# Adapter matmul and quantised FFN: weight units cut by outputs, loop turned by half a period, first two and last sequences re-ordered

## The chip, the cores and the metric

One core of a Trainium2 chip runs the whole kernel. The metric is device time in microseconds (us), from one launch to its end. The core has five engines that run their own instruction streams and meet at semaphores: PE (matmuls; PEld is its weight load), DVE, ACT and POOL (element work), and SP, which here only issues DMAs. SP's queue is in order: an issue that waits holds up all issues behind it.

## What is computed

Eight sequences of 256 tokens, width 1024. Each has its own adapter matrix (1024 x 1024, float32, picked by `itok_B_1_14`), and all share one FFN:

```python
y = einsum('bij,bkj->bik', x, weight[ids])          # adapter: 4 MB of weights per sequence
h = layernorm(y, gamma, beta)
h = fake_quant_int8(h) @ fake_quant_int8(w1).T + b1 # scale per row, round, clip
h = gelu(h)
h = fake_quant_int8(h) @ fake_quant_int8(w3).T + b3
return x + h
```

`fake_quant_int8` divides a row by max|row|/127, rounds, and multiplies back.

## The kernel before

**Adapter matmul.** A float32 product is made of three fp32r matmuls (hi\*hi, lo\*hi, hi\*lo), after both operands are split: `hi` is the value rounded by an ACT copy, `lo` = value - `hi` by DVE (weights) or POOL (tokens). The weights of a sequence come in four units `u` = 0 to 3. `divmod(u, 2)` is `(kh, ch)`: which 512 outputs, which 512 inputs. A unit is 512 outputs x 512 inputs, loaded by four DMAs (`load_unit`, one for 32 partitions each, rows of 128 floats = 512 bytes) into one of two slots of `w_nat`. DVE transposes it in 32 x 32 blocks into PSUM (`transpose_w`, L801) in two pieces `k`, ACT writes `w_hi` (`split_w`, L537), DVE writes `w_lo` (`low_w`, L807), and PE runs piece (u, k): 12 matmuls of 128x512 (`piece`, `products`, L1080 to L1082). The first piece of unit 2 can run when the first piece of that unit is split. Tokens go the same way: `load_x`, `transpose_x` (L816), `split_x`, `low_x` (POOL, L438).

**FFN.** It runs on 128-token tiles t = 0, 1: `copy_y`, `statistics`, `normalisers` (POOL), `normalise` (ACT), `scale_and_shift` (POOL, L413 and L415), `scales_h` (DVE), `round_h` (ACT), `transpose_h` (PE), `take_h`, `ffn1` (16 bf16 matmuls), `rescale1` (DVE, L874), `add_b1` (POOL), `gelu`, `scales_g`, `round_g`, `transpose_g`, `take_g`, `ffn2`, `scale_ffn2` (ACT, L585), `finish` (POOL, L421 and L424), `store`. The products of h and g, and the transposes, share the two banks `f_ps`.

**Preparation.** w1 and w3 are 16 tiles of 128 rows ("prep tiles"), each loaded (`load_prep`), reduced to a row maximum (`max_prep`), rounded (`round_prep`: POOL for tiles 0 to 5, ACT for 6 to 15), transposed by PE (`prepare`) and copied (`take_prep`). The tiles lie in buffers that are borrowed, so some loads wait: tile 13 until 8 tiles are transposed, tiles 14 and 15 until h of sequence 0 is rounded.

**Order.** Everything is written out by hand for each engine. Sequence 0 is transposed by PE (`transpose_first`), not by DVE. Sequences 1 and 2 are written out with the preparation between their pieces. Then a loop over p = 3 to 6 (period p): PE runs units 0 and 1 of sequence p with `ffn2` of p-2 (first half), then units 2 and 3 with `ffn1` of p-1 (second half). DVE and ACT prepare weights half a period ahead: units 2 and 3 of p in the first half, units 0 and 1 of p+1 in the second. Sequence 7 is `last_period`, token tile 0 through all units and then tile 1, before the FFNs of 6 and 7.

In the period SP issues: units 0 and 1 of p+1, store of tile 0, unit 2, store of tile 1, the residual tokens (`load_residual`), tokens of p+2, unit 3. A unit's slot is free when the unit two before it is transposed. A store waits for POOL's `finish`.

## Time and profile before

| | |
|---|---|
| median of 3 runs | 408.69 us (406.43 to 411.79) |
| the profiled execution, device time | 405.16 us |
| its span, first to last instruction | 403.3 us |
| mean granted PE clock | 0.954 of full speed |
| bytes moved | 67.35 MB, mean 167 GB/s |

The profile is of one execution. "Busy" of PE is modelled at its end: matmuls overlap, so the distance between two starts is what one costs, not its printed duration. A row of a timeline is: start, duration, engine, line, operation, tiles, and in brackets how long the engine stood idle before it and on whom it waited.

### The profile page before, as it was taken

The page shows a single profiled execution, that of the slowest core. Times are in us where ns is not written, and L with a number is a line of the kernel's source. Part 1 is how long each engine was busy: PE and PEld are TensorE (multiplying, and loading weights), DVE is VectorE, ACT ScalarE, POOL GpSimd, SP SyncE. Part 2 cuts the span into 40 slices and gives each one's busy share as a digit, 9 for nine tenths or more (in the row PEclk, how much of TensorE's full clock was granted, in tenths as well). Part 3 has the DMA queues.
Part 4 walks back from the last instruction along what each step waited for, and adds up shares of the span by engine and source line. Part 5 has one row for each costly group of instructions (what it writes and reads, how often), then busy time and mean ns, then how long its engine had stood idle before and what let it go on. Part 6 is the DMA issues. An engine that isn't in the chain of part 4 may idle for free. (4 is left out here: it accounts for less than half of the span.)

```text
span 403.3 us, 5528 instructions
## 1 busy us (share of the span) xinstructions
PE 340.1 (84%) x1760; PEld 229.2 (57%) x1760; DVE 292.8 (73%) x348; ACT 237.7 (59%) x248; POOL 266.8 (66%) x160
## 2 busy tenths in 40 slices
PE   3999883988558847899999999999999899992973
PEld 3788663656445533566666666566556566741331
DVE  1489693998776354699768986997689886457457
ACT  2345593858866343786687667756775865214360
POOL 1406334657900647996999699968996899585454
PEclk9999999799888969999999999999999999996898
DMA  7999999964840519999985896689569801300004
GB/s 258 364 265 298 222 283 235 212 160 142 171 105 0 138 20 244 215 191 233 269 154 104 248 250 126 156 257 204 110 156 271 197 0 54 119 37 2 0 27 181
DMA packets 78619, 67.35 MB, mean 167 GB/s; under 512 B 3078, under 2 KB 71686, under 8 KB 78602
## 3 DMA queue, kind: packets, MB, share of 16 engines
q1 hardware_dynamic: 78602, 67.14, 68.9%
q8 instruction: 9, 0.15, 0.2%
q14 instruction: 8, 0.07, 0.1%
HBM read 58.74 MB, written 8.39 MB: 166 GB/s over the span
## 5 line engine op out<-in xcount | busy, mean ns | idle before, releaser
L1080 PE MATMUL a_ps<-w_hi,x_hi 128*128 128x512 f32 x240 | 104.3, 435 | 10.8 <-DVE w_lo L807 8.1
L1129 PE MATMUL f_ps<-w_q,q_t 128*128 128x512 bf16 x416 | 94.3, 380 | 4.9 <-ACT q_t L580 2.7
L1081 PE MATMUL a_ps<-w_lo,x_hi 128*128 128x512 f32 x240 | 96.6, 402 | 0.0
L1082 PE MATMUL a_ps<-w_hi,x_lo 128*128 128x512 f32 x240 | 96.5, 402 | 0.0
L801 DVE STREAM_TRANSPOSE t_ps<-w_nat 128x1024 f32<-128x1024 f32 x56 | 67.3, 1236 | 19.4 <-DMA w_nat<-in_L_cond_weight 19.0
L807 DVE TENSOR_TENSOR w_lo<-t_ps,w_hi 128x1024 fp32r<-128x1024 f32 x56 | 66.9, 1216 | 12.9 <-ACT w_hi L537 12.6
L537 ACT ACTIVATE w_hi<-t_ps 128x1024 fp32r<-128x1024 f32 x56 | 57.1, 1024 | 23.5 <-DVE t_ps L801 22.5
L1129 PEld LDWEIGHTS f_ps<-w_q,q_t 128*128 128x128 bf16 x416 | 38.7, 98 | 55.1 <-issue 4.7
L1080 PEld LDWEIGHTS a_ps<-w_hi,x_hi 128*128 128x128 f32 x240 | 47.1, 196 | 23.9 <-DVE w_lo L807 9.0
L1082 PEld LDWEIGHTS a_ps<-w_hi,x_lo 128*128 128x128 f32 x240 | 46.8, 195 | 10.7
L1081 PEld LDWEIGHTS a_ps<-w_lo,x_hi 128*128 128x128 f32 x240 | 47.2, 197 | 8.7
L438 POOL TENSOR_TENSOR x_lo<-x_t,x_hi 128x1024 fp32r<-128x1024 f32 x14 | 33.5, 2390 | 26.0 <-ACT x_hi L543 26.0
L421 POOL TENSOR_TENSOR o<-o,w_scale_row 128x1024 f32<-128x1024 f32 x12 | 29.6, 2468 | 31.3 <-ACT o L585 31.3
L429 POOL TENSOR_TENSOR x_res<-x_res,rows 128x1024 f32<-128x1024 f32 x14 | 33.9, 2446 | 10.1 <-DMA x_res<-in_x 10.0
L433 POOL TENSOR_TENSOR a<-a,rows 128x1024 f32<-128x1024 f32 x14 | 34.4, 2459 | 8.2 <-DVE a L874 8.2
L850 DVE TENSOR_REDUCE g_max<-a 128x1 f32<-128x1024 f32 x14 | 17.1, 1218 | 18.1 <-ACT a L571 18.1
L424 POOL TENSOR_TENSOR o<-o,x_res 128x1024 f32<-128x1024 f32 x12 | 28.6, 2388 | 0.9
L415 POOL TENSOR_TENSOR y<-y,rows 128x1024 f32<-128x1024 f32 x12 | 28.6, 2386 | 0.9
L413 POOL TENSOR_TENSOR y<-y,rows 128x1024 f32<-128x1024 f32 x12 | 28.6, 2384 | 0.8 <-ACT y L556 0.8
L543 ACT ACTIVATE x_hi<-x_t 128x1024 fp32r<-128x1024 f32 x14 | 14.7, 1052 | 16.0 <-DVE x_t L816 10.6
L842 DVE TENSOR_REDUCE h_max<-y 128x1 f32<-128x1024 f32 x14 | 17.0, 1213 | 9.6 <-POOL y L415 9.6
L575 ACT ACTIVATE a<-a,magic,g_inv 128x1024 f32<-128x1024 f32 x14 | 17.4, 1245 | 10.7 <-DVE g_inv L838 10.7
(143 smaller groups left out, 488.8 us busy)
## 6 DMA issues: line engine op xcount, KB each, us to landing
w_nat<-in_L_cond_weight SPq DMA_DIRECT2D x112, 256.0 KB, 5.5
x_nat<-in_x SPq DMA_DIRECT2D x28, 256.0 KB, 8.1
x_res<-in_x SPq DMA_DIRECT2D x7, 1024.0 KB, 6.9
out<-o SPq DMA_DIRECT2D x14, 512.0 KB, 2.9
w_nat<-in_L_cond_weight SPq DMA_DIRECT2D x4, 512.0 KB, 6.5
w_q<-in_L_ffn_w SPq DMA_DIRECT2D x4, 512.0 KB, 8.7
w_scale_row<-in_L_ffn_w SPq DMA_DIRECT2D x3, 512.0 KB, 9.8
o<-in_x SPq DMA_DIRECT2D x2, 512.0 KB, 4.4
```

Source lines behind the costliest of these rows:

```text
L413: pool.tensor_tensor(row, row, gamma_row, ALU.mult).then_inc(gamma_done, 1)
L421: pool.tensor_tensor(o[:, t, :], o[:, t, :], w_scale_row[:, 1, :], ALU.mult).then_inc(out_scaled, 1)
L429: pool.tensor_tensor(x_res[:, t, :], x_res[:, t, :], b3_row, ALU.add).then_inc(x_b3_ready, 1)
L433: pool.tensor_tensor(a[:, t, :], a[:, t, :], b1_row, ALU.add).then_inc(ffn1_biased, 1)
L438: pool.tensor_tensor(x_lo[:, half], x_t[:, half], x_hi[:, half].bitcast(F32), ALU.subtract).then_inc(x_lo_ready, 1)
L537: act.activation(w_hi[:, u, blocks_of(k)], t_ps[:, k], ACT.Copy).then_inc(w_hi_ready, 1)
L801: dve.transpose(t_ps[:, k].rearrange("p c (kb s) -> p kb c s", s=BLK), w_nat[:, u % 2].rearrange("p kb (c r) -> p kb c r", r=BLK)[:, :, bl ...
L807: dve.tensor_tensor(w_lo[:, u, blocks_of(k)], t_ps[:, k], w_hi[:, u, blocks_of(k)].bitcast(F32), ALU.subtract).then_inc(w_lo_ready, 1)
L1080: pe.matmul(ps, hi, w_hi[:, u, c], start=begin, stop=False)
L1081: pe.matmul(ps, hi, w_lo[:, u, c], start=False, stop=False)
L1082: last = pe.matmul(ps, lo, w_hi[:, u, c], start=False, stop=end)
L1129: last = pe.matmul(ps[:, half, :], q[:, c, :], w[:, c, half_of(half)], start=c == 0, stop=c == CB - 1)
```

## The change

1. **Units cut by outputs.** A unit is now 256 outputs x all 1024 inputs (`LOADED = 256`), still 1 MB in four DMAs, with rows of 256 floats = 1 KB. A piece `k` of it is one half of the inputs. So what PE calls unit (kh, ch) is filled by two loaded units, 2\*kh and 2\*kh+1, and PE waits before it for piece `ch` of the second of them.
2. **Loop turned.** The body begins with the second half: p = 2 to 6, PE runs units 2 and 3 of p with `ffn1` of p-1, then units 0 and 1 of p+1 with `ffn2` of p-1. All engines follow. In SP's cycle the load of unit 1 now stands behind the store of tile 0, and the load of unit 2 behind the residual.
3. **First sequences.** `ffn1` of sequence 0 runs in the first half of sequence 1 (before: in its second half and after), `ffn2` of 0 in the first half of sequence 2 (before: its second). Prep tiles 3 to 8 are transposed between sequences 0 and 1. All rounding is POOL's. The loads are in another order (diff).
4. **Last sequence.** Units 0 and 1 of sequence 7 run in the loop. What is left runs tile 0, tile 1, and the products of 6 and 7 are cut in halves that alternate with transposes. POOL adds b3 to the residual of 6 after `add_b1`, no longer before it. The rounding of h and g of sequence 7 is ACT's, before DVE's.

```diff
-    NK = 2
-    CP = CU // NK
-    PIECES = UNITS * NK
+    CP = CU // 2
+    LOADS = 4
+    PIECES = LOADS * CH
+    LOADED = D // LOADS
+    KB = LOADED // BLK
...
+        def part_of_unit(w, u, k):
+            kh, quarter = divmod(u, LOADS // KH)
+            return w[:, CH * kh + k, :, quarter * LOADED:(quarter + 1) * LOADED]
...
                 for q in range(NQ):
-                    j0 = q * JX + ch * JQ
-                    src = weight[bass.ds(adapter, 1), kh * BANK:(kh + 1) * BANK, j0:j0 + JQ]
+                    src = weight[bass.ds(adapter, 1), u * LOADED:(u + 1) * LOADED, q * JX:(q + 1) * JX]
...
             def period(p):
-                load_unit(p + 1, 0)
-                load_unit(p + 1, 1)
-                store(p - 2, 0)
+                load_residual(p - 1)
                 load_unit(p + 1, 2)
-                store(p - 2, 1)
-                load_residual(p - 1)
                 if not (isinstance(p, int) and p + 2 > LAST):
                     load_x(p + 2)
                 load_unit(p + 1, 3)
+                if not (isinstance(p, int) and p + 2 > LAST):
+                    load_unit(p + 2, 0)
+                store(p - 1, 0)
+                if not (isinstance(p, int) and p + 2 > LAST):
+                    load_unit(p + 2, 1)
+                store(p - 1, 1)
...
             load_first_unit(2)
-            load_first_unit(3)
-            load_prep(range(0, 4))
+            load_prep((0,))
+            load_first_unit(3, (0,))
+            load_prep((1, 2, 5, 3))
             load_x(1)
+            load_first_unit(3, (1,))
+            load_prep((7, 4, 12, 8, 6))
+            load_unit(1, 1)
+            load_prep((9,))
             load_unit(1, 0)
...
+            load_prep((10,))
+            load_x(2)
+            load_prep((11, 13))
             load_unit(1, 2)
...
+            load_prep((14,))
             load_unit(1, 3)
-            load_prep(range(13, 14))
+            load_prep((15,))
+            load_unit(2, 1)
             load_unit(2, 0)
...
             def piece(b, u, k):
+                kh, ch = divmod(u, CH)
...
-                    pe.wait_ge(w_lo_ready, piece_no(b, u, k) + 1)
-                    if u < CH and k == 0:
-                        pe.wait_ge(x_lo_ready, CH * (b - 1) + u + 1)
...
+                elif k == 0:
+                    pe.wait_ge(w_lo_ready, piece_no(b, 2 * kh + 1, ch) + 1)
+                    if kh == 0:
+                        pe.wait_ge(x_lo_ready, CH * (b - 1) + ch + 1)
```

Three places of the order. **SP in the loop, before**: the store of tile 0 (`out<-o`), behind which stands unit 2 of the next sequence.

```order
L321 ISA [waits out_ready]
L321 DMA out<-o 128x1024
L256 TENSOR_LOAD ids_sb
L256 ISA x2
L261 REGISTER_ALU
L266 ISA [waits w_transposed]
L266 DMA w_nat<-in_L_cond_weight 32x16x128
```

**SP in the loop, after**: the same store; what stands behind it is unit 1.

```order
L330 REGISTER_ALU
L332 DMA out<-o 128x1024 [waits out_ready]
L265 TENSOR_LOAD ids_sb
L265 ISA x2
L273 ISA [waits w_transposed]
L273 DMA w_nat<-in_L_cond_weight 32x8x256
```

The load of unit 1 has moved behind a wait for POOL (`out_ready`); the shape of a DMA went from 16 blocks x 128 floats to 8 x 256.

**SP before the loop, after the change**: prep tile 13 with its wait for 8 transposed tiles, and unit 2 of sequence 1 behind it.

```order
L327 DMA o<-in_L_ffn_w 128x1024 [waits first_transposed]
L327 DMA w_scale_row<-in_L_ffn_w 128x1024 [waits wq_transposed]
L265 TENSOR_LOAD ids_sb
L265 ISA x2
L273 ISA [waits w_transposed]
L273 DMA w_nat<-in_L_cond_weight 32x8x256
```

In the kernel before, unit 2 of sequence 1 stood ahead of that tile.

**DVE before the first half of sequence 2, before** (`w_loaded0` and `w_loaded1` are the two slots): unit 0's second piece, then unit 1.

```order
L801 STREAM_TRANSPOSE t_ps<-w_nat 128x16x2x32 [waits w_lo_ready,w_loaded0]
L824 BN_STATS stats<-y 128x6 [waits y_copied] x2
L874 SCALAR_TENSOR_TENSOR a<-f_ps,h_scale,w_scale_row 128x512 [waits ffn1_done,scale_row_ready]
L874 SCALAR_TENSOR_TENSOR a<-f_ps,h_scale,w_scale_row 128x512 [waits ffn1_done]
L831 BN_AGGR mean_var<-stats 128x2 [waits shift_ready,y_stats,consts_ready]
L831 BN_AGGR mean_var<-stats 128x2
L807 TENSOR_TENSOR w_lo<-t_ps,w_hi 128x1024 [waits w_hi_ready]
L801 STREAM_TRANSPOSE t_ps<-w_nat 128x16x2x32 [waits w_lo_ready,w_loaded1]
```

**DVE at the same place, after**: from the first transpose of unit 0 of sequence 2 to the third `w_lo` (the one PE waits for).

```order
L763 STREAM_TRANSPOSE t_ps<-w_nat 128x8x4x32 [waits w_lo_ready,w_loaded0]
L778 STREAM_TRANSPOSE x_t<-x_nat 128x8x8x32 [waits x_lo_ready,x_loaded]
L763 STREAM_TRANSPOSE t_ps<-w_nat 128x8x4x32 [waits w_lo_ready,w_loaded0]
L769 TENSOR_TENSOR w_lo<-t_ps,w_hi 128x4x256 [waits w_hi_ready]
L763 STREAM_TRANSPOSE t_ps<-w_nat 128x8x4x32 [waits w_lo_ready,w_loaded1]
L769 TENSOR_TENSOR w_lo<-t_ps,w_hi 128x4x256 [waits w_hi_ready]
L812 TENSOR_REDUCE g_max<-a 128x1 [waits g_ready]
L798 TENSOR_SCALAR g_scale<-g_max 128x1 [waits g_max_ready]
L800 RECIPROCAL g_inv<-g_scale 128x1 [waits g_scale_ready]
L786 BN_STATS stats<-y 128x6 [waits mean_var_ready,y_copied] x2
L769 TENSOR_TENSOR w_lo<-t_ps,w_hi 128x4x256 [waits w_hi_ready]
```

The token transpose of sequence 2 now stands inside the weight chain, and three `w_lo` instead of one stand before the first piece of the half.

## Rows read from the trace of the kernel before

**Rows 1.** The page: span, busy time of each engine.
```profile
span 403.3 us, 5528 instructions
PE 340.1 (84%) x1760; PEld 229.2 (57%) x1760; DVE 292.8 (73%) x348; ACT 237.7 (59%) x248; POOL 266.8 (66%) x160
```
**Rows 2.** Windows: start:end, length, busy per engine, PE clock, DMA share, GB/s.
```profile
0.00:43.92 43.92, 35.60 (x208) 30.15 (x209) 27.98 (x25) 20.38 (x24) 13.22 (x22) 1.00 1.04 289
43.92:161.73 117.81, 86.71 (x449) 59.92 (x449) 80.69 (x98) 72.72 (x76) 59.55 (x34) 0.90 0.70 160
161.73:317.78 156.05, 152.96 (x770) 101.01 (x769) 129.33 (x158) 109.84 (x113) 136.06 (x72) 1.00 0.88 197
317.78:403.30 85.52, 64.83 (x338) 38.16 (x336) 54.81 (x70) 34.79 (x37) 57.99 (x34) 0.92 0.16 59
182.05:201.01 18.96, 18.96 (x99) 12.66 (x97) 16.21 (x20) 12.43 (x13) 14.76 (x9) 1.00 1.00 254
277.90:298.90 21.00, 19.49 (x98) 12.51 (x96) 15.02 (x20) 14.85 (x17) 20.62 (x13) 1.00 0.71 133
```
**Rows 3.** PE's timeline at two waits and after them (matmul starts).
```profile
71.15 0.79 PE L1080 MATMUL a_ps<-w_hi,x_hi 128*128 128x512 f32 x1 [5.23 <-DVE w_lo L807]
72.17 0.63 PE L1082 MATMUL a_ps<-w_hi,x_lo 128*128 128x512 f32 x1
72.60 0.63 PE L1080 MATMUL a_ps<-w_hi,x_hi 128*128 128x512 f32 x1
121.05 0.77 PE L1080 MATMUL a_ps<-w_hi,x_hi 128*128 128x512 f32 x1 [0.44 <-ACT y L552]
146.83 1.01 PE L1105 MATMUL f_ps<-ident,h_r 128*128 128x128 bf16 x8 [7.02 <-ACT o L585]
230.21 0.39 PE L1082 MATMUL a_ps<-w_hi,x_lo 128*128 128x512 f32 x1
230.44 0.40 PE L1080 MATMUL a_ps<-w_hi,x_hi 128*128 128x512 f32 x1
232.50 0.62 PE L1105 MATMUL f_ps<-ident,h_r 128*128 128x128 bf16 x8
```
**Rows 4.** SP's and DVE's timelines: a store, unit 1 behind it, its transpose.
```profile
135.01 0.37 SPq L321 DMA_DIRECT2D out<-o  x1
136.14 2.00 SPq L266 DMA_DIRECT2D w_nat<-in_L_cond_weight  x4
143.37 1.26 DVE L801 STREAM_TRANSPOSE t_ps<-w_nat 128x1024 f32<-128x1024 f32 x1 [8.68 <-DMA w_nat<-in_L_cond_weight]
```
**Rows 5.** DMA packets in the stretches 0:20, 10:15, 20:22, 23.5:28.5, 29:33 us.
```profile
DMA packets 5024, 6.19 MB, mean 310 GB/s; under 512 B 184, under 2 KB 4280, under 8 KB 5024
DMA packets 1751, 1.74 MB, mean 349 GB/s; under 512 B 61, under 2 KB 1747, under 8 KB 1751
DMA packets 228, 0.82 MB, mean 410 GB/s; under 512 B 28, under 2 KB 28, under 8 KB 228
DMA packets 1253, 1.08 MB, mean 216 GB/s; under 512 B 66, under 2 KB 1250, under 8 KB 1252
DMA packets 1548, 0.85 MB, mean 213 GB/s; under 512 B 50, under 2 KB 1525, under 8 KB 1548
```
**Rows 6.** DVE's timeline in the loop: `w_lo` of units 3, transposes of unit 1, rescale.
```profile
217.81 2.35 DVE L807 TENSOR_TENSOR w_lo<-t_ps,w_hi 128x1024 fp32r<-128x1024 f32 x2
228.19 2.34 DVE L801 STREAM_TRANSPOSE t_ps<-w_nat 128x1024 f32<-128x1024 f32 x2
230.44 1.37 DVE L874 SCALAR_TENSOR_TENSOR a<-f_ps,h_scale,w_scale_row 128x512 f32<-128x512 f32 x2
```
**Rows 7.** POOL's timeline in the same period: the end of `finish` of tile 0.
```profile
218.64 2.37 POOL L424 TENSOR_TENSOR o<-o,x_res 128x1024 f32<-128x1024 f32 x1
```
**Rows 8.** POOL's timeline at the end: the residual of 6, then `add_b1`.
```profile
354.56 5.64 POOL L429 TENSOR_TENSOR x_res<-x_res,rows 128x1024 f32<-128x1024 f32 x2 [6.37 <-DMA x_res<-in_x]
361.27 3.33 POOL L433 TENSOR_TENSOR a<-a,rows 128x1024 f32<-128x1024 f32 x1
```

709 lines of the change are left out of this document (305 added, 404 removed).

## The prediction, made before the changed kernel ran

> **What bounds the kernel now.** I first read the page and then windows cut where PE starts a sequence. PE is busy 84% of the span and no other engine more than 73% [rows 1], but that is a mean over four stages [rows 2]. 0 to 43.9: sequence 0, filled by DMA. 43.9 to 161.7: sequences 1 and 2 among the preparation, 117.8 us with PE busy 86.7 and a granted clock of 0.90. 161.7 to 317.8: the loop, four periods in 156.1 us, PE busy 153.0. 317.8 to 403.3: the last sequence and the last FFNs, 85.5 us with PE busy 64.8.
>
> The loop has little to give. An undisturbed half period is 18.96 us [rows 2], four products and four transposes of FFN and 48 matmuls at the distance of two starts, 0.23 us [rows 3]. Four periods at 2 x 18.96 are 151.7; 156.1 were measured, so all waits of the loop are 4.4 us. The gain or loss of this change has to come from the second and fourth stage. There PE waits for DVE's `w_lo`, and DVE for loads: 5.23 us at 71.15, and 7.02 at 146.83 [rows 3]. The second is a chain through SP's queue: the store of sequence 0 goes out at 135.01, unit 1 of sequence 3 behind it at 136.14, and its transpose starts at 143.37 after 8.68 us of idle DVE [rows 4]. After such waits PE's clock is at its lower level (1.2 GHz): two matmuls start 0.43 us apart (72.17 and 72.60) where 0.23 is usual (230.21 and 230.44) [rows 3]. Over the 12 matmuls of a piece that is 2.4 us, so a wait of 5 us costs 7.4.
>
> **The 1 KB runs.** Here the title's first item is weighed. In 23.5 to 28.5 us the queue moved tokens, whose form is exactly that of the new weight loads (32 partitions, 8 blocks of 256 floats): 216 GB/s. In 29 to 33 us it moved weight units in 512-byte runs: 213 GB/s. Runs of 1 KB to 128 partitions (10 to 15 us) went at 349, and prep tiles in 4 KB rows at 410 (20 to 22) [rows 5]. The new loads stay with 32 partitions per DMA, so I take the row of the same form: 1.05 MB at 216 GB/s is 4.9 us a unit, as before (4.9). The bound on the other side is 349 GB/s, 3.0 us. From issue to transpose an isolated unit takes 7.2 us (136.14 to 143.37) [rows 4], 2.0 of it issuing.
>
> The Trainium skill, page "DMA: Bandwidth & Descriptors", section Specifications, gives 512 B as the smallest transfer for line rate, so by it too going from 512 B to 1 KB buys nothing. By the page the sum below stands as it is; by the 349 row it would be some 6 us lower, which is a rival below. The trace agrees with the page for loads of this form (216 against 213), not for what is line rate: 4 KB rows went at twice that.
>
> **The first sequences, step by step.** Before 20 us about the same bytes go out (6.19 MB) [rows 5]. Then the new queue holds, ahead of and including unit 0 of sequence 1: prep 5 and 3 (0.52 MB each, 1.28 us at 410), tokens (4.9), half a first unit (1.5 at 349), five prep tiles (6.4), unit 1 (4.9), prep 9 (1.3), unit 0 (4.9). That is 26.5 us, so unit 0 has landed at about 47.5 with 1 us of latency. Unit 0 used to come before four of those tiles, so sequence 1 starts later than at 43.9. PE needs three `w_lo`: DVE does three transposes and three `w_lo` at 1.17 each (two in 2.34 or 2.35) [rows 6] and 1.5 of statistics: 47.5 + 8.5 = 56.0. Between, PE transposes prep tiles 3 to 8. The clock is then low: +2.4.
>
> The first half of sequence 1 now carries `ffn1` of 0: 18.96 + 0.9 for the scale row + 2.4 = 22.3, to 78.3. The second half is four pieces of 2.75 (12 x 0.23) = 11.0, with seven prep transposes of 0.45 and a scale row: 15.1, to 93.4. But DVE is late for sequence 2. From 56.0 it has five transposes and three `w_lo` (9.4), three prep maxima (3.5), two `scales_h` (3.0), a rescale and a scale (1.8), and about 0.8 of waiting for units, until unit 3 of sequence 1 is transposed at 74.5. Only then is SP let on to unit 1 of sequence 2, and unit 0 stands behind it although its slot has been free: 74.5 + 1.3 + 2 x 4.9 = 85.6, about 86. From there to the third `w_lo` the order shows three weight transposes and three `w_lo` (7.0), the token transpose (2.3), `scales_g` (1.5) and statistics (1.3): 12.1. PE starts sequence 2 at 98.2, after 5 us of idling, again at the low clock. With `ffn2` of 0 inside, the half takes 18.96 + 2.4, and I add 0.9 for hand-overs: the second half of sequence 2 starts at **120.5**. POOL, which now rounds all tiles, is not the limit in this sum: beside the rounding it has 20 instructions of some 2.4 us [rows 7] between 45 and 120, and its tightest point, `low_x` of sequence 2, comes out at 95.6 against 98.2.
>
> Before, PE reached that place at 121.05 [rows 3]. The same time, but in another state: `ffn2` of 0 is done, and the loop is entered. From 121.05 the old kernel needs 40.7 us to the start of sequence 3 at 161.73. The new one needs a half period, 18.96 + 0.4: sequence 3 starts at 139.9. **First part: -21.8 us.**
>
> **The loop.** All engines keep their cyclic order, with two exceptions. PE's first piece of unit 2 waits for a third `w_lo` instead of a first. Before, that `w_lo` (the first of the pair that starts at 217.81 [rows 6]) was done at 219.0, and PE came to the place at 219.97, the end of a half of 18.96 from 201.01 [rows 2]: 1.0 us to spare, so it costs nothing, but nothing is left as cover. Second, unit 1 stands behind the store of tile 0. POOL's `finish` ends at 221.01 [rows 7]; with 0.4 for the store and 7.2 to the transpose, unit 1 is there at 228.6, and DVE wants it at 228.19 [rows 6]. The transposes, then the rescale, slip 0.4 to 0.7; the rescale ended at 231.8 and PE wants the bank at 232.50 [rows 3, 6], so most of it is swallowed. In front of the residual unit 1 takes the place of unit 2, so the residual lands no later. I take 39.4 for a period, 0.4 over the 39.0 measured: four periods 157.6 against 156.1, sequence 7 starts at 297.5. **+1.5 us.** Bounds: 37.9 a period (-4.5) and 42.0, twice the worst half [rows 2] (+12).
>
> **The last stage.** It was 85.5 us. POOL's queue stood 6.37 us for the residual of 6 and spent 5.64 on it [rows 8], ahead of the normalisers of the last tile and of `add_b1` (361.27), on which both FFNs hung: 12.0, now moved behind. The halved products that alternate with transposes I count at 1.0. 85.5 - 13.0 = 72.5. **-13.0 us.** Bounds: 0, if something else arrives as late as POOL did, and -20.7, all of the stage's time with PE idle.
>
> **Sum.** 403.3 - 21.8 + 1.5 - 13.0 = 370.0 us of span. Around the span lie 1.9 us (405.16 device time), so 371.9, a ratio of 0.918 to that execution. The median of the runs is 408.69, so I expect **375 us**.
>
> **Rivals.**
> *Unit 1 behind the store paces the loop* (0.18). Then POOL's `finish`, the landing, the rescale and PE's transpose form a ring, and the 0.4 to 0.7 of each period adds up with the missing cover before unit 2: a half of 21.0 occurred [rows 2]. At 2 us per period over mine, five periods in all: +10, **385 us**. For it: the ring made the 7.02 us wait. Against it: in the loop only 0.4 us are missing.
> *The new runs go at 349 GB/s* (0.12). A unit takes 1.9 us less. Two units lie in a row before sequence 2 (-3.8, to which the low clock adds), and unit 1 is in time in the loop (-1.6): **369 us**. Against it: the token row.
> *The gain in front is lost again* (0.06). The new order is right only if each engine finds its operands; the old one lost 31 us of PE in its second stage. If the ordered queues lose 20 us of the 21.8, it ends near **396**, and a little more gives no change.
> *Slower* (0.03). A unit takes long from issue to transpose because of its 32-partition form. The price is paid at each load behind a released slot: four in front and one in each of five periods. It decides from 4.6 us each: 9 x 4.6 = 41 over 375 is 2% above 408.69. Against it: 7.2 us were measured where the queue was free, and the queue is 12% idle in the loop [rows 2]. **420 us**.
>
> **How the numbers follow.** The forecast has 0.61 and by itself 367 to 383: the loop's lower bound, and 8 us for steps left out of the hand-made chain. To hold 8 in 10 the range takes in both nearer rivals: 364 to 392. About 2% is what a measurement can tell from no change. Faster by over 2% means below 400.5: forecast, the first two rivals, and two thirds of the third, 0.93, less a little for a mechanism I don't see: 0.91. Same 0.05, slower 0.04.
>
> **What would show it.** Right: unit loads still near 215 GB/s; sequence 1 starts near 56 and sequence 2 near 98, each after a wait for `w_lo` and with matmuls 0.43 apart; sequence 3 near 140; periods of 39 to 40; a last stage of 72 without POOL waiting for a residual. Wrong: a `w_nat` load that DVE waits for in every period, PE waiting for `w_lo` ahead of unit 2 each time, or POOL busy without a gap from 45 to 120 with PE waiting for `x_lo`.

## The result, and the profile after

The changed kernel takes 390.5 us (median of 4 runs, 390.23 to 393.73), the kernel before 409.07 in the same comparison: a ratio of 0.956, 95% interval 0.948 to 0.964. Its profiled execution took 390.59 with a span of 388.7. The direction held, and so did the range (364 to 392), by 1.5 us; 375 was expected. The forecast of the span was 370.0, so 18.7 us of the gain of 33.3 did not come. For the runs below: on the chip of t1, d1 and d2 the kernel before took 403.3 to 415.3 us, and seven of its eleven executions there were in a slower state at a lower granted clock, so the record calls the ratios of these three unclear. The page of after, against [rows 1]:

```profile
span 388.7 us, 5553 instructions
PE 336.1 (86%) x1732; PEld 227.5 (59%) x1760; DVE 287.2 (74%) x345; ACT 230.0 (59%) x241; POOL 278.2 (72%) x170
```

The busy times moved little: PE 4.0 us less, DVE 5.6 less, ACT 7.7 less and POOL 11.4 more, since all the rounding of the preparation is now POOL's. Nearly the same work stands closer together. The windows are cut at the same places as [rows 2] (start of sequence 1, 3 and 7); columns: start:end, length, busy per engine with counts, PE clock, DMA share, GB/s.

```profile
0.00:64.91 64.91, 42.23 (x249) 35.01 (x249) 36.51 (x38) 26.48 (x29) 22.94 (x33) 0.90 1.01 259
64.91:150.62 85.71, 76.99 (x406) 53.96 (x409) 69.84 (x84) 56.99 (x62) 60.78 (x33) 0.96 0.76 179
150.62:309.90 159.28, 153.22 (x755) 100.95 (x769) 128.77 (x157) 107.93 (x113) 137.23 (x73) 1.00 0.80 185
309.90:388.70 78.80, 63.62 (x332) 37.55 (x336) 52.05 (x69) 38.60 (x40) 57.25 (x34) 0.94 0.21 72
```

| | before | forecast | measured | off by |
|---|---|---|---|---|
| sequence 3 starts | 161.73 | 139.9 | 150.62 | +10.7 |
| four periods | 156.05 | 157.6 | 159.28 | +1.7 |
| last stage | 85.5 | 72.5 | 78.8 | +6.3 |

So the first part gave 11.1 where 21.8 was forecast, the loop lost 3.2 where 1.5 was, and the last stage gave 6.7 where 13.0 was. I read each of the three.

**The front.** PE's and DVE's timelines around the start of sequence 1 (forecast: unit 0 landed at 47.5, start 56.0):

```profile
58.99 1.01 PE L1044 MATMUL f_ps<-ident,w_scale_row 128*128 128x128 bf16 x8 [8.39 <-ACT w_q L598]
64.14 1.01 PE L1044 MATMUL f_ps<-ident,a 128*128 128x128 bf16 x8 [1.99 <-ACT w_q L598]
64.91 0.77 PE L1018 MATMUL a_ps<-w_hi,x_hi 128*128 128x512 f32 x1
66.33 0.63 PE L1018 MATMUL a_ps<-w_hi,x_hi 128*128 128x512 f32 x1
66.76 0.63 PE L1019 MATMUL a_ps<-w_lo,x_hi 128*128 128x512 f32 x1
55.61 1.26 DVE L763 STREAM_TRANSPOSE t_ps<-w_nat 128x1024 f32<-128x1024 f32 x1 [3.94 <-DMA w_nat<-in_L_cond_weight]
61.93 2.41 DVE L769 TENSOR_TENSOR w_lo<-t_ps,w_hi 128x1024 fp32r<-128x1024 f32 x2
```

Unit 0 of sequence 1 comes at 55.61, 8.1 us late, and the start is 8.9 late. PE's printed wait is not for `w_lo` but for a prep tile that ACT should copy (8.39). The third `w_lo` is done at 64.34 (61.93 + 2.41), 0.6 before the start, so the rows alone don't say which of the two chains holds. The matmuls behind it are 0.43 apart (66.33, 66.76), PE's lower level of 1.2 GHz, as before [rows 3].

The next sequence, in SP's and DVE's timelines:

```profile
86.99 4.39 SPq L273 DMA_DIRECT2D w_nat<-in_L_cond_weight  x8
99.07 1.26 DVE L763 STREAM_TRANSPOSE t_ps<-w_nat 128x1024 f32<-128x1024 f32 x1 [4.92 <-DMA w_nat<-in_L_cond_weight]
```

Units 1 and 0 of sequence 2 go out together at 86.99, in the sum at 74.5, and the transpose of unit 0 comes 12.1 us behind; 11.5 was the sum. Sequence 2 starts at 111.11, forecast 98.2. These 12.9 us are 8.9 at the start of sequence 1, 3.6 from there to the transpose of its unit 3 (22.1 us in place of 18.5) and 0.4 behind it. The 3.6 are waits of DVE for units 2 and 3 (1.81 at 71.04, 2.89 at 82.99; 0.8 in the sum). SP and DVE, for unit 3:

```profile
72.86 0.36 SPq L327 DMA_DIRECT2D y_first<-in_L_ffn_w  x1
73.97 1.81 SPq L273 DMA_DIRECT2D w_nat<-in_L_cond_weight  x4
82.99 1.26 DVE L763 STREAM_TRANSPOSE t_ps<-w_nat 128x1024 f32<-128x1024 f32 x1 [2.89 <-DMA w_nat<-in_L_cond_weight]
```

The slot of unit 3 is free at 65.5, when unit 1 is transposed. Its load goes out only at 73.97, because prep tile 14 (72.86) stands ahead of it in SP's queue and waits until the first tile of h of sequence 0 is rounded (done at 72.83).

**The loop.** One period, SP, DVE and PE (compare [rows 4] and [rows 6]):

```profile
252.08 1.84 SPq L273 DMA_DIRECT2D w_nat<-in_L_cond_weight  x4
259.94 2.39 DVE L763 STREAM_TRANSPOSE t_ps<-w_nat 128x1024 f32<-128x1024 f32 x2 [1.77 <-DMA w_nat<-in_L_cond_weight]
262.24 1.37 DVE L836 SCALAR_TENSOR_TENSOR a<-f_ps,h_scale,w_scale_row 128x512 f32<-128x512 f32 x2
263.66 0.62 PE L1044 MATMUL f_ps<-ident,h_r 128*128 128x128 bf16 x8 [1.10 <-DVE a L836]
```

Unit 1 goes out behind the store, is there 7.9 us later (7.2 in the sum), DVE has waited 1.77, the rescale slips and PE waits 1.10. The store itself left 1.14 us ahead of the unit (250.94; the sum had 0.4 between them). This is the worst of the four periods: in the other three the unit is there after 7.3 us, DVE waits 1.2 and PE 0.5. The 1.1 behind the store is the same in all.

**The last stage.** DVE, POOL, PE and ACT:

```profile
339.44 1.30 DVE L881 SCALAR_TENSOR_TENSOR y<-y,rstd,rows 128x1024 f32<-128x1024 f32 x1 [0.66 <-POOL rstd L407]
346.15 3.32 POOL L441 TENSOR_TENSOR a<-a,rows 128x1024 f32<-128x1024 f32 x1
347.30 3.25 DVE L881 SCALAR_TENSOR_TENSOR y<-y,rstd,rows 128x1024 f32<-128x1024 f32 x1
353.52 0.62 PE L1044 MATMUL a_ps<-ident,h_r 128*128 128x128 bf16 x8 [2.62 <-ACT h_r L568]
356.23 1.04 ACT L577 ACTIVATE a<-a 128x1024 f32<-128x1024 f32 x1
362.32 1.21 DVE L812 TENSOR_REDUCE g_max<-a 128x1 f32<-128x1024 f32 x1
365.25 0.62 PE L1044 MATMUL t_ps<-ident,a 128*128 128x128 bf16 x8 [3.75 <-ACT a L581]
```

POOL waits for no residual of 6 any more, and the bias that stood behind it comes 36.3 us into the stage (346.15 from 309.90), before 43.5 (361.27 [rows 8] from 317.78). That is 7.2 us and not 12.0. From that bias to the end it is 42.6 us, before 42.0, so the halved products gave nothing. PE waits twice behind the bias: 2.62 for `h_r`, where DVE's step on y took 3.25 in place of 1.30 beside POOL, and 3.75 for g, where the GELU was done at 357.3 and DVE took its maximum at 362.32, behind four operations of its queue.

### The profile page after: what moved, and what is told of

Its sections match the earlier page's. It is cut to its first block, busy times and chain, and to the rows that moved or that the text cites. A ratio compares the mean times of both kernels' runs of the same rounds, so it can differ in the third digit from the quotient of the medians.

```text
span 388.7 us, 5553 instructions
## 1 busy us (share of the span) xinstructions
PE 336.1 (86%) x1732; PEld 227.5 (59%) x1760; DVE 287.2 (74%) x345; ACT 230.0 (59%) x241; POOL 278.2 (72%) x170
## 3 DMA queue, kind: packets, MB, share of 16 engines
HBM read 58.74 MB, written 8.39 MB: 173 GB/s over the span
## 4 chain that ended last, share of the span: by engine, by line
POOL 38%; issue 16%; PE 8%; DVE 6%; ACT 2%; POOLq 0%; ACTq 0%
POOL x_lo L446 7%; POOL y L421 7%; POOL o L429 6%; POOL x_res L437 6%; POOL a L441 4%; POOL y L423 4%; POOL o L432 3%; PE f_ps L1069 3%; PE t_ps L1069 1%; POOL rstd L407 1%; PE a_ps L1018 1%; DVE x_t L929 1%; PE a_ps L1019 1%; PE a_ps L1020 1%; DVE y L881 1%
## 5 line engine op out<-in xcount | busy, mean ns | idle before, releaser
L1018 PE MATMUL a_ps<-w_hi,x_hi 128*128 128x512 f32 x256 | 109.6, 428 | 2.0 <-ACT y L552 1.2
L1020 PE MATMUL a_ps<-w_hi,x_lo 128*128 128x512 f32 x256 | 101.8, 398 | 0.0
L1019 PE MATMUL a_ps<-w_lo,x_hi 128*128 128x512 f32 x256 | 101.8, 398 | 0.0
L1069 PE MATMUL f_ps<-w_q,q_t 128*128 128x512 bf16 x375 | 88.8, 380 | 5.7 <-ACT q_t L586 3.1
L1069 PEld LDWEIGHTS f_ps<-w_q,q_t 128*128 128x128 bf16 x400 | 37.1, 98 | 52.4 <-ACT q_t L586 6.4
L1018 PEld LDWEIGHTS a_ps<-w_hi,x_hi 128*128 128x128 f32 x256 | 49.6, 194 | 15.9 <-ACT y L552 3.1
L1020 PEld LDWEIGHTS a_ps<-w_hi,x_lo 128*128 128x128 f32 x256 | 49.2, 192 | 11.2
L1019 PEld LDWEIGHTS a_ps<-w_lo,x_hi 128*128 128x128 f32 x256 | 49.6, 194 | 9.1
L446 POOL TENSOR_TENSOR x_lo<-x_t,x_hi 128x1024 fp32r<-128x1024 f32 x14 | 33.6, 2401 | 22.1 <-ACT x_hi L543 21.9
L429 POOL TENSOR_TENSOR o<-o,w_scale_row 128x1024 f32<-128x1024 f32 x14 | 33.3, 2377 | 11.1 <-ACT o L591 11.1
L432 POOL TENSOR_TENSOR o<-o,x_res 128x1024 f32<-128x1024 f32 x14 | 33.7, 2409 | 1.1
L423 POOL TENSOR_TENSOR y<-y,rows 128x1024 f32<-128x1024 f32 x12 | 28.7, 2396 | 0.9
```

Of the source, the lines that this page charges most:

```text
L429: pool.tensor_tensor(o[:, t, :], o[:, t, :], w_scale_row[:, 1, :], ALU.mult).then_inc(out_scaled, 1)
L446: pool.tensor_tensor(x_lo[:, half], x_t[:, half], x_hi[:, half].bitcast(F32), ALU.subtract).then_inc(x_lo_ready, 1)
L1018: pe.matmul(ps, hi, w_hi[:, u, c], start=begin, stop=False)
L1019: pe.matmul(ps, hi, w_lo[:, u, c], start=False, stop=False)
L1020: last = pe.matmul(ps, lo, w_hi[:, u, c], start=False, stop=end)
L1069: last = pe.matmul(ps[:, half, :], q[:, c, :], w[:, c, half_of(half)], start=c == 0, stop=c == CB - 1)
```

## The experiments

Twelve kernels (m_rates, which only measures loads, is not in the table), each an edit of the changed one unless it says otherwise. The ratio is to the kernel before, run on the same chip; they come from several chips, so ratios compare better than times. The four middle columns are PE's starts in the profiled execution.

| run | us | ratio (95%) | seq. 1 / its 2nd half | seq. 2 | 4 periods | last stage |
|---|---|---|---|---|---|---|
| the changed kernel | 390.5 | 0.956 (0.948 to 0.964) | 64.9 / 88.0 | 111.1 | 159.3 | 78.8 |
| a2_prep_first | 390.9 | 0.955 (0.950 to 0.960) | 62.5 / 85.3 | 108.4 | 161.8 | 80.4 |
| a3_unit0_first | 388.5 | 0.947 (0.941 to 0.953) | 57.7 / 86.2 | 107.2 | 159.6 | 82.1 |
| a4_swap_seq2 | 386.0 | 0.945 (0.941 to 0.948) | 61.9 / 85.0 | 103.4 | 159.1 | 80.1 |
| a6_tokens_late | 392.6 | 0.959 (0.951 to 0.966) | 62.0 / 85.5 | 108.3 | 159.8 | 78.8 |
| c1_front | 385.6 | 0.941 (0.933 to 0.950) | 57.0 / 85.7 | 103.5 | 160.8 | 80.5 |
| b1_unit_before_store | 382.3 | 0.933 (0.923 to 0.942) | 61.3 / 83.6 | 106.0 | 155.6 | 79.9 |
| b3_residual_late | 390.1 | 0.952 (0.945 to 0.960) | 63.5 / 86.3 | 108.3 | 160.3 | 79.0 |
| t1_tail | 389.4 | 0.962 (0.955 to 0.969) | 61.8 / 84.0 | 105.6 | 159.9 | 78.4 |
| d1_swap_store | 379.7 | 0.937 (0.930 to 0.944) | 63.8 / 86.7 | 105.1 | 154.0 | 79.9 |
| d2_all | 371.4 | 0.915 (0.910 to 0.919) | 58.3 / 84.0 | 102.5 | 154.0 | 77.0 |
| f1_act_tail | 369.9 | 0.900 (0.896 to 0.905) | 57.7 / 81.2 | 99.7 | 154.0 | 74.2 |

The table first shows a spread. The changed kernel, b1, b3, t1 and m_rates have the same front, word for word, and start sequence 2 at 111.1, 106.0, 108.3, 105.6 and 108.8. They come from several chips; b1 and b3 ran on one and are 2.4 apart. The profile that I read above is the latest of five; their mean is 108.0. About 3 of the 12.9 us by which sequence 2 was late are this spread, and no single profile of an edit to the front may be read to better than 2 or 3 us.

### The form of the loads

This kernel loads, after its last store, 2.1 MB in each of four forms, twice over, and waits after each (471.7 us in all, 82 of them from the first added load on).

```diff
+            for form in (0, 1, 2, 3, 0, 1, 2, 3):
+                for u in range(2):
...
+                sp.wait_ge(last_stored, 16 * (TT * KH + n))
```

> The changed kernel, and after its last store eight more stretches of loads with nothing else on the queue (the output is unaffected; only what runs before them is the kernel). Each stretch loads two weight units (2.1 MB) into the two slots and waits for them: 512-byte runs to 32 partitions per DMA (the old form), 1 KB runs to 32 partitions (the new form), 1 KB runs to 128 partitions, 4 KB rows to 128 partitions, then the four again. My step of the prediction (the run's length buys nothing, the 32 partitions are what costs): 215 GB/s, about 10 us, for both of the first two, 350 and 410 GB/s for the others. Rival (1 KB runs are faster in themselves, and in the kernel something else slows them): the second form well over the first, near 350. Rival (the new form is slower than the old, since a partition is written in 8 pieces by the same few engines): second form at 150 to 190 GB/s, as in the start of the changed kernel, against 215.

DMA packets in the middle of four stretches: 512-byte runs to 32 partitions, 1 KB to 32, 1 KB to 128, 4 KB rows to 128.

```profile
DMA packets 3345, 1.66 MB, mean 221 GB/s; under 512 B 104, under 2 KB 3345, under 8 KB 3345
DMA packets 1895, 1.83 MB, mean 228 GB/s; under 512 B 112, under 2 KB 1895, under 8 KB 1895
DMA packets 1546, 1.49 MB, mean 298 GB/s; under 512 B 93, under 2 KB 1546, under 8 KB 1546
DMA packets 432, 1.58 MB, mean 394 GB/s; under 512 B 47, under 2 KB 47, under 8 KB 432
```

The step stands: 221 and 228, and 218 and 226 in the second round. From one form's first issue to the next form's went 11.7 us for each of the two (387.58, 399.26, 410.97). Longer runs to 32 partitions buy nothing that this kernel shows; what costs is the 32 partitions, since the same 1 KB runs to 128 went at 298. That is less than the 350 expected, so the row of 349 in [rows 5] was not the rate of that form in another place. The Trainium skill, page "SBUF — State Buffer", section "Door 1: The DMA port swizzle (why `[64,N]` ≈ `[32,N]`)", says that partitions 0 to 31 reach only 8 of the 16 memory ports, with about 218 GB/s as the limit. The trace is at that figure or up to 5% above it, with 218 to 228 (394 for 4 KB rows to all 128).

### The start of sequence 1: prep tiles, or the load

```diff
+            take_prep((4, 5))
             split_w(1, 0, 0)
-            take_prep((4, 5))
...
+            round_prep((7, 8))
             normalisers_of(0)
-            round_prep((7, 8))
```

> Changed kernel; only ACT's copy of prep tiles 4 and 5 goes ahead of the first w_hi of sequence 1, and POOL's rounding of tiles 7 and 8 ahead of the first normalisers. They are what PE idles for at 58.99 (8.39 us) and to 64.14. Theory A (unit 0 of sequence 1 lands late; the tiles wait behind it but are not the bound): the wait for the tiles goes, a wait for w_lo takes its place, sequence 1 starts at 64.3 in place of 64.9, and the whole is the same within 1 us (390). Theory B (the queues of ACT and POOL are the bound): sequence 1 starts at 57 to 58, and the whole gets 6 us less (384).

PE and DVE in that run:

```profile
50.99 0.61 PE L1044 MATMUL f_ps<-ident,w_scale_row 128*128 128x128 bf16 x8 [0.31 <-ACT w_q L598]
61.74 1.01 PE L1044 MATMUL f_ps<-ident,a 128*128 128x128 bf16 x8 [10.14 <-ACT w_q L598]
62.52 0.78 PE L1018 MATMUL a_ps<-w_hi,x_hi 128*128 128x512 f32 x1
59.54 2.40 DVE L769 TENSOR_TENSOR w_lo<-t_ps,w_hi 128x1024 fp32r<-128x1024 f32 x2
```

Tiles 6 and 7 are now transposed by 51.0, 8 to 10 us sooner, and nothing is won: 390.9. The wait went to tile 8 (10.14), and sequence 1 starts 0.6 behind its `w_lo` (59.54 + 2.40 = 61.94), as before the edit. The largest printed wait of this place, 8.39, was worth nothing. That is as theory A has it: both chains stand behind the load. The run with another order of loads, next, shows it.

```diff
-            load_unit(1, 1)
-            load_prep((9,))
             load_unit(1, 0)
-            load_prep((10,))
+            load_unit(1, 1)
+            load_prep((9, 10))
...
-            max_prep((9,))
...
-            max_prep((10, 11))
+            max_prep((9, 10, 11))
             scales_h(0, 0, 0)
```

> Changed kernel; only the loads of sequence 1 in another order: unit 0, unit 1, prep tiles 9 and 10, in place of unit 1, tile 9, unit 0, tile 10 (DVE's maximum of tile 9 goes back to those of 10 and 11). Theory A (the landing of unit 0 starts the chain): unit 0 is transposed at about 47.5 in place of 55.6, the third w_lo then waits for unit 1, which lands near 53, so sequence 1 starts at 57 to 59 (6 to 8 us earlier); at the end 384, if sequence 2 follows, since its loads wait for slots that come free with sequence 1. Theory B (sequence 2 has its own bound in the store and load queue): sequence 1 starts at 58, sequence 2 again at 111, the whole 390.

DVE, PE:

```profile
65.30 1.22 DVE L820 TENSOR_REDUCE wq_max<-o 128x1 f32<-128x1024 f32 x1 [4.75 <-DMA o<-in_L_ffn_w]
69.36 1.04 PE L1042 MATMUL f_ps<-ident,h_r 128*128 128x128 bf16 x8 [3.17 <-ACT h_r L561]
```

Unit 0 is transposed at 47.47, as the theory had it (DVE no longer waits for it), and sequence 1 starts at 57.7, where the forecast had 56.0. But its second half starts at 86.2, no sooner than in a2 (85.3): all of the start's gain is gone, since DVE now waits 4.75 us for prep tile 11 (in `o`; its load stands behind the tokens of sequence 2) ahead of the scales of h, and PE 3.17 for h. Sequence 2 starts at 107.2, inside the spread of 105.6 to 111.1. Theory A had the start right, theory B the end. The reason that B gave, the queue of stores and loads, is not what the rows show ahead of the second half.

```diff
             load_prep((10,))
-            load_x(2)
             load_prep((11, 13))
             load_unit(1, 2)
+            load_x(2)
```

> Changed kernel; only the load of sequence 2's tokens (1 MB, issued at 43.6 while unit 0 of sequence 1 is under way) goes behind unit 2 of sequence 1. In the two other profiles of the same front part unit 0 is transposed at 52.7 to 53.2 and sequence 1 starts at 62 (in that of the changed kernel itself 55.6 and 64.9). Theory A (transfers issued after unit 0 share its engines and hold it up, which a sum over what stands ahead of it in the queue does not see): unit 0 is transposed at 49 to 50, sequence 1 starts at 58.5. Theory B (the queue is in order, so later issues cost nothing; the loads are only slower than 216 GB/s): unit 0 is transposed at 52 to 53 again. The whole: 387 to 389 by A, 390 by B.

Unit 0 is transposed at 52.74, inside the 52.0 to 55.6 of the five profiles with the old order (52.74 in m_rates), and not at 49 to 50. So nothing shows that what is issued later holds it up (one profile, against a spread of 3.6 us), and my sum over what stands ahead in the queue was the right kind of sum. What was wrong is the rate. The sum ahead of unit 0 held 7.9 MB after 20 us in 26.5 us, 297 GB/s. In the changed kernel the stretch 20 to 52 us moved this:

```profile
DMA packets 4947, 8.08 MB, mean 252 GB/s; under 512 B 340, under 2 KB 3859, under 8 KB 4945
```

At 252 those 7.9 MB need 31.3 us in place of 26.5, 4.8 of the 8.1 us; in the fastest of the same fronts (b1, 271 GB/s, transpose at 52.0) 29.2, 2.7 of 4.5. The rest is the landing itself and the spread. The mixture of forms need not be the reason. In 24 to 28 us the queue holds nearly only the tokens, one form; here in the changed kernel and in b1:

```profile
DMA packets 727, 0.71 MB, mean 178 GB/s; under 512 B 42, under 2 KB 723, under 8 KB 727
DMA packets 860, 0.84 MB, mean 210 GB/s; under 512 B 51, under 2 KB 856, under 8 KB 860
```

The five profiles have 178, 189, 201, 210 and 212 there, and the kernel before 215: one form of load already runs at different rates in different executions, up to 18% under the sum's 216. Why is open.

### Sequence 2: the order of its units

```diff
-            load_unit(2, 1)
             load_unit(2, 0)
+            load_unit(2, 1)
```

> Changed kernel; only unit 0 of sequence 2 is loaded ahead of unit 1 of it, whose slot comes free later. Theory A (the queue held unit 0 back 8 to 9 us for nothing): unit 0 is issued at 78, DVE transposes it without a wait at 94.2 in place of 99.07, the third w_lo is done at 106.2; but POOL's x_lo of sequence 2 stands behind the residual, whose load is issued as late as before, and is done at 108.7, so sequence 2 starts at 108.9 in place of 111.1, waiting for x_lo: 388. Theory B (the landing takes over at unit 1 instead, which then comes 4 us later): sequence 2 starts at 111 or later, 390 to 392.

```profile
90.97 1.25 DVE L763 STREAM_TRANSPOSE t_ps<-w_nat 128x1024 f32<-128x1024 f32 x1
103.39 0.47 PE L1018 MATMUL a_ps<-w_hi,x_hi 128*128 128x512 f32 x1
```

DVE (first row) finds unit 0 without a wait, PE (second) starts sequence 2 at 103.4, 5.0 before a2 on the same chip, and all of it is kept to the end: 386.0 against 390.9. It gave more than expected, since the load of the residual moved forward too and POOL's `x_lo` wasn't late. The order that the prediction described ("unit 0 stands behind it although its slot has been free") cost 5 us of whole time.

### The front once more

```diff
+            load_unit(1, 0)
             load_unit(1, 1)
-            load_prep((9,))
-            load_unit(1, 0)
-            load_prep((10,))
-            load_x(2)
-            load_prep((11, 13))
+            load_prep((9, 10, 11, 13))
             load_unit(1, 2)
+            load_x(2)
...
-            max_prep((10, 11))
             scales_h(0, 0, 0)
+            low_w(1, 1, 1)
+            max_prep((9, 10))
             transpose_w(1, 2, 0)
-            max_prep((12,))
-            low_w(1, 1, 1)
...
             low_w(1, 2, 0)
+            max_prep((11, 12))
             rescale1(0, 0)
```

> Changed kernel with all of the front: unit 0 of sequence 1 first, then unit 1, tiles 9, 10, 11, 13, unit 2, tokens of 2; DVE's maxima of 9 to 12 behind the scales of h and the fourth w_lo of sequence 1 (in the run with unit 0 first, the maximum of tile 10 held DVE 4.75 us and with it h of 0, and the 4.3 us gained at the start of sequence 1 were gone at its second half: 86.2); ACT's and POOL's prep tiles ahead; unit 0 of sequence 2 ahead of unit 1. Theory A (each of these waits hid the next, and together they go): sequence 1 starts at 55 to 57, its second half at 78 to 80, sequence 2 at 98 to 99, as I had forecast; the whole 381. Theory B (DVE and ACT have no room between 56 and 98, since they carry the preparation too): sequence 2 starts at 102 to 103, as with the swap alone; the whole 385 to 386.

DVE and PE:

```profile
65.56 1.22 DVE L767 TENSOR_TENSOR w_lo<-t_ps,w_hi 128x1024 fp32r<-128x1024 f32 x1 [5.45 <-ACT w_hi L535]
77.66 1.01 PE L1041 MATMUL f_ps<-ident,h_r 128*128 128x128 bf16 x8 [4.50 <-DVE a L834]
```

DVE waits for no weight load in sequence 1 now, and its second half still starts at 85.7: the `w_lo` waits 5.45 for ACT, which stands behind the scale row and h, and PE waits 4.50 for a rescale that stands behind two maxima. Sequence 2 is at 103.5, what the swap alone gives. So far theory B.

### The loop: unit 1 and the store

```diff
                     load_unit(p + 2, 0)
-                store(p - 1, 0)
-                if not (isinstance(p, int) and p + 2 > LAST):
                     load_unit(p + 2, 1)
+                store(p - 1, 0)
                 store(p - 1, 1)
```

> Changed kernel; only SP's order in the loop and before it: unit 1 of the next sequence goes ahead of the store of tile 0, no longer behind it. Its slot is free 5.7 us before the store goes out (transpose done at 245.2, store at 250.94). Theory A (unit 1 behind the store costs the periods their excess over 39.0): DVE's wait for w_nat (1.77 at 259.94) and PE's for the rescale (2.6 in four periods) go, the four periods take 156.5 in place of 159.3, the whole 387.5. Theory B (the excess is ACT's and POOL's chain: PE waits 0.29 for the copy of y and 0.38 for g in each period, and the rest is not at this wait): the rescale wait goes but the four periods stay at 158.5 to 159.3, the whole within 1 us of 390.

PE's waits in the four periods, summed by what it waited for; first the changed kernel:

```profile
PE f_ps L1044 <- DVE a L836: 2.6, 4, 1.1
PE f_ps L1069 <- ACT q_t L586: 1.4, 4, 0.4
PE a_ps L1018 <- ACT y L552: 1.2, 4, 0.3
```

then with the unit first:

```profile
PE f_ps L1068 <- ACT q_t L585: 1.5, 3, 0.8
PE a_ps L1017 <- ACT y L551: 0.9, 4, 0.3
```

The wait for the rescale is gone, and the four periods take 155.6 in place of 159.3 to 160.3: 38.9 each. In d1, d2 and f1, which have this order too, they take 154.0, that is 38.5. So theory A, and its price is 3.7 to 5.3 us in four periods, more than the printed 2.6: between two starts PE lost 0.65, 0.67, 0.69 and 1.25 at the rescale, 3.3 in all, and 1.3 of the 4.6 that it loses around the copy of y (7.3 between two starts where 6.1 is undisturbed) went with it. That is 4.6, of which b1 gives back about 1 in the first half of sequence 3 (21.1 us in place of 20.1); d1, d2 and f1 don't. The whole time fell by 7.8 us (390.1 of b3 on the same chip to 382.3). The two profiled executions are 6.0 apart: 4.7 in the loop, 2.3 in the front, which is the same code and so spread, and 1.0 the other way in the last stage.

### The last stage

```diff
             normalisers(LAST, slice(0, 1))
-            residual_last(0)
...
             add_b1(f, 0)
-            residual_last(1)
             add_b1(f, 1)
...
             residual(f)
+            residual_last(0)
+            residual_last(1)
```

> Changed kernel; only POOL's order at the end: its three residual additions (b3 on the tokens of 7, twice, and on those of 6) all go behind the bias of a. DVE's operation on y took 3.25 us at 347.30 beside POOL's additions, and 1.30 at 339.44 without. Theory A (DVE and POOL slow each other when both work from SBUF, and POOL is kept by a load from 339.7 to 344.9): y takes 1.3 to 2.3, h of the last tile is rounded 1.5 to 2.5 us sooner, g of 6 starts to be scaled sooner; the last stage 76.5 in place of 78.8, the whole 388. Theory B (PE's products and ACT's chain set the end, POOL only fills idle time): same within 1 us, 390. The additions could also come beside DVE's last ones and give it back: 390 to 392.

```profile
344.35 3.32 POOL L441 TENSOR_TENSOR a<-a,rows 128x1024 f32<-128x1024 f32 x1 [1.49 <-DVE a L836]
345.50 3.25 DVE L881 SCALAR_TENSOR_TENSOR y<-y,rstd,rows 128x1024 f32<-128x1024 f32 x1
```

The same pair collides: it was POOL's bias, not its residuals, and the stage stays at 79.0. This edit does not test what the collision costs. The next keeps it and changes DVE's order:

```diff
                 last_statistics(1)
-                rescale1(f, 0)
                 last_h(1)
+                rescale1(f, 0)
...
+                scales_g(f, 1, a[:, 1, :], 1)
                 rescale_and_bias_half(0)
                 rescale_and_bias_half(1)
-                scales_g(f, 1, a[:, 1, :], 1)
```

> Changed kernel; only the end: DVE makes h of the last tile ahead of the rescale of (6, 0), and the scales of g of (6, 1) ahead of the rescale and bias of the last tile, where in the changed kernel they stood behind and ACT was ready 5 us earlier (gelu done at 357.3, maximum at 362.32); POOL's three residual additions last, as in the run before. PE waits 2.62 for h_r at 353.52 and 3.75 for a at 365.25. Theory A (DVE's queue order makes both waits: y comes beside POOL's bias and takes 3.25, g stands behind four operations): both go to under 1, and the last stage is 73 to 75 in place of 78.8; the whole 385 to 387. Theory B (the waits are only the slack of a chain of ACT and DVE over the last tile, which is as long in any order): they move to later transposes, the stage stays at 77 to 79, the whole 389 to 391.

ACT, PE:

```profile
346.97 1.06 ACT L577 ACTIVATE a<-a 128x1024 f32<-128x1024 f32 x1 [5.33 <-POOL a L441]
349.22 0.62 PE L1044 MATMUL a_ps<-ident,h_r 128*128 128x128 bf16 x8 [3.45 <-ACT h_r L568]
```

Theory A had it that DVE's order makes both waits. DVE's step on y takes 1.30 again and `h_inv` is ready at 343.2, but PE waits 3.45: ACT's queue has the GELU of (6, 0) ahead of the rounding of h and stands there 5.33 us for POOL. POOL's bias comes 39.9 us into the stage in place of 36.3, since the rescale that it waits for now stands behind h. The stage is 78.4, no gain. The whole time (384.9 to 391.4 in five executions) does not tell the theories apart; the stage does, and the waits moved, as theory B has it. Whether they had to is asked by the last run.

### The orders together

> Changed kernel with the two orders of SP that each gained alone: unit 0 of sequence 2 ahead of unit 1, and unit 1 ahead of the store in the loop. Alone: sequence 2 started 5.0 us earlier (108.4 to 103.4, whole 386.0), and four periods took 155.6 in place of 159.3 (whole 382.3). Theory A (two separate waits, in separate stages): sequence 2 at 101 to 103.5, four periods 155 to 156, the whole 377 to 379. Theory B (part of what the second gained in whole time is not the loop's, and the spread of the front part between executions is 2 to 3 us): the stages as by A, but the whole 380 to 381, which is 390.5 less 5.0 and 4.3.

The periods are 154.0, below what both had. Sequence 2 starts at 105.1 and not by 103.5; sequence 1 began at 63.8 in this profile, 1.9 later than in a4, so the swap's gain is there (41.3 from one start to the other, 41.5 in a4, 45.9 in a2). The whole of 379.7 lies between A and B, and the interval of the ratio takes in both: undecided, and of no weight for the rest.

d2_all adds t1's order, ACT's `scale_ffn2(f, 1)` ahead of its last copy, and the front of c1 with this order of DVE (and the fourth `split_w`, then both `round_h(0, t)`, sooner on ACT):

```diff
-            max_prep((10, 11))
             scales_h(0, 0, 0)
+            low_w(1, 1, 1)
+            max_prep((9,))
+            scales_h(0, 1, 1)
             transpose_w(1, 2, 0)
-            max_prep((12,))
-            low_w(1, 1, 1)
-            scales_h(0, 1, 1)
             transpose_w(1, 2, 1)
             low_w(1, 2, 0)
             rescale1(0, 0)
+            max_prep((10,))
+            low_w(1, 2, 1)
             transpose_w(1, 3, 0)
-            low_w(1, 2, 1)
+            max_prep((11, 12))
```

> Both orders of SP, the end of the first of these runs with ACT's scale of (6, 1) ahead of its last copy, and a front laid out once more: unit 0 of sequence 1 first, h of sequence 0 ahead of the maxima of tiles 9 to 12 on DVE, and the fourth w_hi ahead of the scale row on ACT. In the first try of the front PE waited 4.50 us for the rescale behind two maxima, and sequence 1's second half began at 85.7 as ever. Theory A (the half is held by the places of single operations): second half at 80 to 82, sequence 2 at 98 to 100; four periods 155 to 156; the last stage 72 to 75; the whole 368 to 373. Theory B (from 57 on, the chain of h of sequence 0 through POOL and ACT needs its 28 us in any order): second half at 84 to 86, sequence 2 at 103; the whole 373 to 377.

371.4 us, which is theory A's range. But the second half of sequence 1 starts at 84.0 and sequence 2 at 102.5, which is what theory B had, and the last stage takes 77.0, where A had 72 to 75. The reason isn't B's chain of h: PE waits 2.54 us for `w_lo` at 84.04, and DVE 2.63 for unit 3 at 77.83, whose load went out at 67.39 behind prep tile 14. In the next run, the same program up to there, DVE waits 0.41 for it and the half starts at 81.2, so theory A isn't excluded either. That run adds only ACT's order at the end:

```diff
-                gelu(f, 0)
                 round_h_last(1)
                 take(h_transposed, TT * LAST + 2, a_ps[:, 1], q_last[:, 0, 1], h_t_ready)
+                gelu(f, 0)
...
                     act.activation(part, part, ACT.Gelu).then_inc(last_half_gelu, 1)
-                take(g_transposed, TT * f + 2, t_ps[:, 0, 0], q_t[:, 1], g_t_ready)
+                    if half == 0:
+                        take(g_transposed, TT * f + 2, t_ps[:, 0, 0], q_t[:, 1], g_t_ready)
```

> The kernel before this one with one more edit, ACT's order at the end: the rounding and copy of h of (7, 1) go ahead of the GELU of (6, 0), and the copy of g of (6, 1) between the two halves of the last GELU. In the run with DVE's new order PE still waited 3.46 for h_r: h_inv was ready 3.7 us before ACT came to it, because ACT stood at the GELU for POOL's bias. Theory A (the queues of the end hold each other one after the other, and with ACT's order the wait at last goes): the wait for h_r under 1, from the second half of 7 to the end 54.5 to 56 in place of 58.0, the whole 368 to 370. Theory B (the chain of bias, GELU, maximum and rounding of 6 and 7 is the length of the stage): the wait comes back at the transpose of g of (6, 0), the stage stays at 57 to 58, the whole 371 to 372.

The window of its last stage, and PE's two largest waits there:

```profile
292.70:366.90 74.20, 62.04 (x332) 37.00 (x336) 51.68 (x67) 38.33 (x40) 55.66 (x33) 0.99 0.23 79
PE t_ps L1042 <- ACT w_nat L666: 2.7, 1, 2.7
PE a_ps L1042 <- ACT a L578: 1.5, 1, 1.5
```

The wait for `h_r` is gone, another of 1.5 came for g of (6, 0), and one of 2.7 near the end. From the second half of 7 to the end it is 55.1 us in place of 58.0: theory A in size, with theory B's returning wait in part. The clock of the stage is 0.99 where it was 0.94 in the changed kernel and 0.92 before [rows 2]. The whole is 369.9, 0.900 of the kernel before (0.896 to 0.905). That is only 1.5 less than d2's on another chip, though the two profiled spans are 5.7 apart (372.6 and 366.9): d2's profile is the slowest of its six executions, and the front, where nothing was changed, was 2.8 us sooner in f1's. The stage's 2.9 is read from one profile of each.

## Why the prediction was right in kind and 18.7 us off in size

**The range held in part by luck.** The forecast by itself was 367 to 383; 390.5 lies in the range only because it was widened for the rivals. The first of them (385) took the loop's cost right in kind, but only 1.7 us of the miss are the loop's. The rival nearest to what happened is the third, "the gain in front is lost again" (0.06): 10.7 of its 21.8 us were. Of the signs, "a `w_nat` load that DVE waits for in every period" is one that was to mean wrong, and it came: 1.2 to 1.8 us in all four. The chances were added wrongly, too: forecast, first two rivals and two thirds of the third are 0.95, not 0.93.

**Right.** The bound: the gain came from the second and fourth stage and not from the loop. The 1 KB runs: 221 against 228 GB/s alone. The cover ahead of unit 2 "costs nothing": in no period of the loop does PE wait for `w_lo`. The clock after the wait of sequence 1: 0.43 between matmuls. The second half of sequence 2, 131.25 to 150.62: 19.4, as forecast. That POOL with all the rounding is not the limit of the front: PE waits for tiles that POOL rounds 1.40, 0.55 and 1.11 us there, and moving tiles 7 and 8 ahead gave nothing.

**The sum ahead of unit 0** (forecast 47.5, measured 55.6, in five profiles 52.0 to 55.6). This step failed by its size, 8.1 us of the 12.9 at sequence 2 in this profile. The kind of sum holds (a6). Its rates came from one execution and from stretches of 2 to 5 us; over 32 us the loads went at 252 to 271 GB/s where the sum had 297. I also took a row's best figure, 410, for every prep tile (394 alone in m_rates).

**"The first half of sequence 1 takes 22.3 us from its start."** It did in the changed kernel (23.1), because the start was late. With the start at 57 to 58 it took 23.5 to 28.7 in four other kernels (a3, c1, d2, f1). From c1 to d2 it fell from 28.7 to 25.7, and the edits only moved DVE's maxima behind the scales of h and ACT's fourth `w_hi` and h forward; f1, the same front as d2, has 23.5, with unit 3 there sooner. So these queues set it, in which h of sequence 0 and the prep tiles stand between the weights, SP's among them. I had added up one engine's instructions, DVE's, and taken the others as ready. This is the other step that failed. In the changed kernel it shows in the second half, 23.1 us where the sum had 19.9: sequence 2 was late because units 2 and 3 of sequence 1 made DVE wait 1.81 and 2.89 us, 0.8 in the sum, unit 3 behind the wait of prep tile 14. No run moves that load ahead of the tile, so what it would give is not shown. The low clock that I had added for sequence 2 did not come (20.1 in place of 22.3), since PE ended its preparation just ahead of it.

**The loop** (+1.7). "Most of it is swallowed" was wrong: the issue was 1.1 and not 0.4 us behind the store in every period, and the slip went through the rescale to PE. [rows 4] had that 1.13 already (135.01 to 136.14). The 7.2 from issue to transpose held in three of four periods (7.3) and was 7.9 in one. The first rival had the mechanism right and the price wrong: 0.9 to 1.3 us a period, not 2 over my sum. With the unit ahead of the store a period is 38.5 to 38.9, less than the 39.0 of before.

**The last stage** (+6.3). The term of 12.0 counted POOL's wait and work in full. Only 7.2 came off POOL's bias, which now hangs on DVE's rescale (done at 346.07), and that on PE's products: 4.8 of the 6.3. The halved products were counted at 1.0 and gave -0.5, the other 1.5: with them three orders (DVE, ACT, POOL) had to fit, and didn't. Orders could also make up for most of the miss: the orders of DVE and ACT with the earlier scale, together, gave 5.7 us (79.9 in d1, 74.2 in f1), near all of the 6.3. t1 shows that DVE's order alone gives none of it.

Put together, the best kernel starts sequence 3 at 138.7, needs 154.0 for the periods and 74.2 for the end: 366.9 of span, where the forecast had 139.9, 157.6 and 72.5. The prediction was of a kernel in which each queue finds its next operand in time; the changed one had places on SP, DVE and ACT where it doesn't. Which share each single place has in the front is not told apart: c1 to f1 changed several at once, within a spread of 2 to 3 us.

## What to carry to other kernels

Where work is ordered by hand on five queues, an estimate from one engine's instructions is the time that the best order could give; take from it what the waits of the second engine in line will hold back, here about half. Before acting on the largest printed wait, ask when the other operand of that instruction was ready: 8.39 us here were worth nothing, because the `w_lo` came only 0.6 us sooner than the start. Behind a store an engine's load inherits the wait of that store; a load whose buffer is free goes ahead of it. The same holds behind a load that waits, as prep tile 14 did here.
